# Attention kernel: value products in bursts of three steps, maximum products of two heads on row halves of the array

## What is computed

```python
q = jnp.einsum('bsd,hdk->bhsk', x, wq)
k = jnp.einsum('bsd,hdk->bhsk', x, wk)
v = jnp.einsum('bsd,hdk->bhsk', x, wv)
scores = jnp.einsum('bhsk,bhtk->bhst', q, k) / jnp.sqrt(jnp.asarray(K, x.dtype))
probs = jax.nn.softmax(scores, axis=-1)
o = jnp.einsum('bhst,bhtk->bhsk', probs, v)
...
return jnp.einsum('bse,ed->bsd', concated, head_kernel)
```

## Time and profile before

| | |
|---|---|
| median of 3 runs | 5213.08 us (5210.68 to 5217.73) |
| the profiled execution, its span | 5214.6 us |
| PE busy | 4965.0 us (95%) |
| DVE busy | 3832.6 us (73%) |
| POOL busy | 2796.0 us (54%) |
| ACT busy | 2665.8 us (51%) |
| granted TensorE clock, mean | 0.980 |

### The profile page before, as it was taken

The page is one execution under the profiler, slowest core; times in us unless marked ns, Lnnn a source line. Parts: engine busy times, 40 slices in busy tenths (PEclk is TensorE's granted clock), DMA queues, the critical chain, the costliest instruction groups (busy, mean ns, idle before and its releaser), DMA issues. The chain is left out here.

```text
span 5214.6 us, 92843 instructions
## 1 busy us (share of the span) xinstructions
PE 4965.0 (95%) x25829; PEld 3227.2 (62%) x25829; DVE 3832.6 (73%) x8495; ACT 2665.8 (51%) x6408; POOL 2796.0 (54%) x1611
## 2 busy tenths in 40 slices
PE   5999999999999999999999999999999999999997
PEld 3556666666566666666666666666666656666666
DVE  5667768677776777777777776777867777677765
ACT  2664555555544545545455455455455554554542
POOL 0665555555555555555555555555555555555652
PEclk7999999999999999999999999999999999999998
DMA  1000000000000000000000000000000000000000
GB/s 39 6 10 7 6 16 6 11 7 6 16 6 10 7 10 11 6 11 11 10 6 6 10 11 11 7 6 16 6 11 7 6 16 6 10 6 10 6 1 14
DMA packets 43025, 49.54 MB, mean 10 GB/s; under 512 B 26256, under 2 KB 34311, under 8 KB 42503
## 3 DMA queue, kind: packets, MB, share of 16 engines
q1 hardware_dynamic: 42503, 43.12, 2.7%
HBM read 23.45 MB, written 19.09 MB: 8 GB/s over the span
## 5 line engine op out<-in xcount | busy, mean ns | idle before, releaser
L1155 POOL TENSOR_TENSOR sums<-sums,probs 128x736 f32<-128x736 f32 (+3 forms) x1344 | 2384.6, 1774 | 1278.0 <-ACT probs L867 1262.6
L867 ACT ACTIVATE probs<-scores 128x368 f32<-128x368 f32 (+3 forms) x3456 | 1460.1, 474 | 1922.0 <-PE scores L761 1814.5
L925 DVE TENSOR_REDUCE part_max<-work 128x1 f32<-128x368 f32 (+3 forms) x3456 | 1657.3, 527 | 310.1 <-PE work L675 288.3
L778 PE MATMUL o_ps<-probs,values 128*64 128x368 f32 (+1 forms) x6912 | 1455.7, 500 | 0.0
L759 PE MATMUL scores<-q_a,k_a 128*128 128x368 f32 (+3 forms) x3456 | 1170.2, 339 | 61.1 <-issue 41.5
L761 PE MATMUL scores<-q_b,k_b 128*128 128x368 f32 (+3 forms) x3456 | 1146.4, 332 | 0.0
L675 PE MATMUL work<-k_a,q_a 128*128 128x368 f32 (+3 forms) x3456 | 1089.6, 378 | 48.0 <-DVE part_max L925 24.4
L675 PEld LDWEIGHTS work<-k_a,q_a 128*128 128x128 f32 (+1 forms) x3456 | 578.3, 184 | 777.4 <-issue 624.1
L1151 POOL TENSOR_TENSOR sums<-probs 128x736 f32<-128x736 f32 (+1 forms) x192 | 343.6, 1789 | 863.5 <-ACT probs L867 861.5
L759 PEld LDWEIGHTS scores<-q_a,k_a 128*128 128x128 f32 (+1 forms) x3456 | 639.5, 185 | 83.8 <-issue 33.2
L761 PEld LDWEIGHTS scores<-q_b,k_b 128*128 128x128 f32 (+1 forms) x3456 | 641.3, 186 | 53.0 <-issue 33.7
(11 more groups left out here) (186 smaller groups left out, 5039.6 us busy)
## 6 DMA issues: line engine op xcount, KB each, us to landing
resid_rows<-h_in SPq DMA_DIRECT2D x16, 576.0 KB, 2.8
h_out<-resid_rows SPq DMA_DIRECT2D x16, 576.0 KB, 4.1
h_in<-in_pe_table_dram SPq DMA_DIRECT2D x16, 512.0 KB
out_dram<-h_out SPq DMA_DIRECT2D x16, 512.0 KB
q_b<-max_rows SPq DMA_DIRECT2D x128, 4.0 KB
q_b<-max_rows SPq DMA_DIRECT2D x128, 0.3 KB
counts<-in_x_dram SPq DMA_DIRECT2D x16, 116.0 KB, 3.0
out_raw<-n_expert_out_weight_dram SPq DMA_DIRECT2D x1, 1024.0 KB
```

Source lines behind the costliest of these rows:

```text
L778: mm = nc.tensor.matmul(o_ps[64 * i:64 * i + 64, 0:cw], values[0:n, t, h * DH:(h + 1) * DH], probs[0:n, s % NP, i, 0:cw], start=(t == 0), ...
L867: nc.scalar.activation(probs[0:n, s % NP, i, 0:cw], scores[0:n, h % SB, 0:cw], ACT.Exp, scale=DH ** -0.5).then_inc(probs_ready, 1)
L925: nc.vector.tensor_reduce(part_max[0:n, i * NT + j, c:c + 1], w[0:n, 0:keys], AX.X, ALU.max).then_inc(drained[k], 1)
L1155: nc.gpsimd.tensor_tensor(acc, acc, probs[0:n, s % NP, :, 0:cw], ALU.add).then_inc(sums_done, 1)
```

## The change

- **Bursts.** `weigh` is no longer done in each step, but at every third step for the three steps before, twelve records in a row (`BURST`). `probs` has 5 buffers for that: the first two steps of a group of three alternate between two buffers each, the third always has the fifth.
- **Maxima in pairs.** A unit `max` is now both heads of a query tile and a key chunk: head 0 on rows 0 to 63 of the array, head 1 on rows 64 to 127, with the high parts alone, into two neighbouring banks. DVE reads both with one reduction (27 for each pair of heads in place of 54). `q_a` of the second head is laid out with its halves exchanged, so that its high part is in rows 64 to 127.
- **Their places.** Maxima no longer fill in: the three key chunks of one query tile stand at every third step, two units in front of the burst, one behind it (and behind a `sum`, which stands right after the burst). They start at step 15 of the pair before the one ahead. For every three query tiles there is now a `maxrow` and its own DMAs (2, 2 and 4 for the three groups), and `score` waits at the first step of each chunk for those groups that it needs.
- **Banks.** The four banks are given to the unit that finds one longest unused; a `max` takes banks 0 and 1 or 2 and 3.
- **Rest.** `qk` stands at every second step, `sum` one step later, ACT's copy of `o_ps` one step later; `h_in` shares memory with the last pair's `heads_t`, and `beats` with `logits`, to make room.

```diff
+SLOTS = LANES + LANES // 2
-NP = 3
+NP = 5
+GROUP = 3
-MAXROW = 23
+BURST = ("burst",)
+MAX_FIRST, MAX_EARLY = 15, 2
+MAX_DMAS = (2, 2, 4)
...
-LOAD = {"v": (48, 0, 36), "qk": (48, 95, 130), "max": (16, 50, 0), "maxrow": (10, 50, 0), "sum": (65, 0, 36),
+LOAD = {"v": (48, 0, 36), "qk": (48, 95, 130), "max": (17, 91, 0), "maxrow": (10, 50, 0), "sum": (65, 0, 36),
...
+    first = STEPS * (p - 1) + MAX_FIRST
+    return [(first + NT * g + GROUP * k, ("max", p, g, 3 * g + k, c))
+            for g in range(NC) for k in range(3) for c in range(NC)]
+
+
+def max_rows_at(p, g):
+
+    return STEPS * (p - 1) + MAX_FIRST + NT * g + 2 * GROUP + 2
...
-            put(NT * (q + 1) + 2, ("sum", q))
+            put(NT * (q + 1) + 3, ("sum", q))
...
+def in_order(units, burst):
+
+    pairs = [u for u in units if u[0] == "max"]
+    sums = [u for u in units if u[0] == "sum"]
+    others = [u for u in units if u[0] not in ("max", "sum")]
+    early = MAX_EARLY if burst else 0
+    return pairs[:early] + [BURST] * burst + sums + pairs[early:] + others
...
+            if u[0] == "max":
+                lane = min((0, 2), key=lambda k: max(used_at[k:k + 2]))
+                slot, lanes = LANES + lane // 2, (lane, lane + 1)
+            else:
+                lane = min(range(LANES), key=lambda k: used_at[k])
+                slot, lanes = lane, (lane,)
...
+    def slot(s):
+
+        return s // GROUP % 2 * 2 + s % GROUP if s % GROUP < GROUP - 1 else NP - 1
+
+    def held(s):
+
+        return GROUP if s % GROUP == GROUP - 1 else 2 * GROUP
...
-                mm = nc.tensor.matmul(w[0:n, 0:cw], q_a[p % 2][i][:, j * P:j * P + n],
-                                      k_a[p % 2][i][:, c0:c0 + cw], start=True, stop=True)
+                for i in range(2):
+                    rows_i = slice(DH * i, DH * i + DH)
+                    mm = nc.tensor.matmul(work[0:n, seg.lane[u] + i, 0:cw], q_a[p % 2][i][rows_i, j * P:j * P + n],
+                                          k_a[p % 2][i][rows_i, c0:c0 + cw], start=True, stop=True)
...
-            if s % STEPS == 0:
-                pe.wait_ge(max_loaded, 64 * (PAIRS * b + p + 1))
+            if t == 0:
+                pe.wait_ge(max_loaded, 16 * sum(MAX_DMAS) * (PAIRS * b + p) + 16 * sum(MAX_DMAS[:c + 1]))
...
+        def weigh(seg, it, b, s):
+
+            for done in range(s - GROUP, s):
+                weigh_one(seg, it, b, done)
...
-                wait(act, probs_used, ALL * b + s - NP + 1)
-                if not isinstance(b, int) or b > 0 or s >= NP:
-                    wait(act, sums_done, (NT - 1) * PAIRS * NC * b + summed(s - NP))
+                back = held(s)
+                wait(act, probs_used, ALL * b + s - back + 1)
+                if not isinstance(b, int) or b > 0 or s >= back:
+                    wait(act, sums_done, (NT - 1) * PAIRS * NC * b + summed(s - back))
...
-                nc.vector.tensor_reduce(part_max[0:n, i * NT + j, c:c + 1], w[0:n, 0:keys], AX.X,
+                lane = seg.lane[u]
+                nc.vector.tensor_reduce(part_max[0:n, :, j, c], work[0:n, lane:lane + 2, 0:keys], AX.X,
                                         ALU.max).then_inc(drained[k], 1)
```

212 lines of the change are left out of this document (112 added, 100 removed).

## The result

| | before | after |
|---|---|---|
| median, us | 5213.48 | **5619.76** (5617.80 to 5633.43) |
| profiled execution: span, us | 5214.6 | 5617.3 |
| PE busy | 4965.0 (95%) | 4780.4 (85%) |

The changed kernel takes 1.0784 times as long, 95% interval 1.0768 to 1.0799: 7.8% slower, where 5.7% faster was forecast, and outside the range. PE is busy for 185 us less and is done 403 us later.

What follows compares the result with a forecast made beforehand. The prediction took PE, busy 95%, to bound the kernel: 5214.6 - 477 of work on PE + 180 of waits = 4918, and 4916 us as the median lies 1.5 lower. The range was 4790 to 5100.

Steps and rivals of the forecast that it cites:

- Work on PE: All of PE's products and shape switches: 442 - 230 + 279 - 14 = 477 us off, 30 us an item.
- The visit's 0.35 us: Value products and sums on column halves: 0.15 us to enter, 0.20 to leave; 1264 fewer visits, 442 us off.
- the switches of 0.20 on either side: Full array to row halves and back around a burst: at least 0.40 us a burst, 230 us on over 576 bursts.
- the pair's overlap: Maximum products: both row halves run at once, a pair takes 0.175 us; 279 us off.
- rival 1: Weights of the row halves come one after another, pairs 0.22 us and bursts at 0.62; 5086 us; chance 15%.
- rival 4: Slower: the row halves don't overlap, a pair takes 0.336 us and the shape is dear; 5267 us; chance 6%.
- the gate's wait: Steps 21 to 27 of an item: PE waits 4.5 us for DVE, busy with the gate's chain and pairs' reductions.
- Together 12 us an item, 180 in all: Sum of new waits of PE, over 15 items with the full mix: gate 4.5, DVE elsewhere, DMAs, scores.
- DVE elsewhere: DVE late behind an embedding, an expert or a projection's four subtractions: 3 us an item, from none to 6.
- scores 2.5: In otherwise empty steps PE outpaces ACT's exponentials (0.67 against 0.84 us): eight groups or so, 0.3 each, an item.
- The DMAs' 2: Scores wait for the rows of maxima to be copied and land: 2 us an item, from none to 4.
- rival 2: DVE and the DMAs bind more: waits of 23 us an item in place of 12; 5086 us; chance 12%.

Runs made afterwards that it cites:

- e4: The changed kernel with DVE's reduction of a pair of maxima reading only 46 of the 368 keys; 5455 us.
- e10: The changed kernel with the pair's reduction reading an eighth of the keys and ACT's exponential taking only the first half of the queries; 5397 us.
- e6: The changed kernel with bursts of three steps kept, but maxima as before the change, and half of a burst step's units ahead of the burst; 5242 us.
- e13: Against e6: four bursts in nine steps (of 3, 2, 2 and 2 steps) in place of three, the plan's load of a burst in proportion; 5190 us.
- e7: The changed kernel with value products of one step at every step again, pairs of maxima still at every third step; 5835 us.
- e16: The changed kernel with its pairs of maxima one to a step in place of three at each third step, the maxima's row written one step later; 5691 us.
- e17: Against e16: the bursts and even plan of e15 besides, so pairs of maxima stand one to a step; 5621 us.
- e15: Against e6: four bursts in nine steps (of 3, 2, 2 and 2 steps), and the plan counts 80 at each step; 5140 us.
- e18: Against e15: ten of an item's twelve sums stand one step later, right behind a burst; 5162 us.
- e14: Against e6: the plan counts 80 at each step in place of 240 at each third, bursts unchanged; 5227 us.
- e1: The changed kernel with one pair of maxima in front of a burst and two behind it; 5489 us.
- e2: The changed kernel with all three pairs of maxima behind the burst; 5691 us.
- e8: The changed kernel with one pair ahead of a burst, projections moved to burst steps where they may be, and put ahead of the burst there; 5392 us.
- e12: Against e6: all other units of a burst step put ahead of the burst; 5273 us.

## Why the prediction was wrong

- **Work on PE: right.** 477 us off forecast, 488 measured. The visit's 0.35 us, the burst's 2.0, the switches of 0.20 on either side, the pair's overlap (some 4 ns between its ends) and its 0.37: each within 0.02 us. Rivals 1 and 4 are refuted by the pair's records. (In rival 1, 1728 pairs of 0.22 are 380 us and not 387, so its time would be 5079; nothing rests on it.)
- **The single costs that I worked out for other engines: right too.** A pair's reduction 0.9 us (911 ns); the gate's wait 4.5 (4.0, a group earlier).
- **The waits: wrong, and this is the step that failed.** "Together 12 us an item, 180 in all" was 750 us, and 900 with the clock. Its terms by item, against measured ones, which hold the low clock of their places: DVE elsewhere 3, against some 31 (35 more in front of maxima, less the gate's 4); scores 2.5, against 16; value products, which had no term, 5. The low clock had no term either and is 10 of these (150 over 15 items). The DMAs' 2 came to nothing: the weight loads of the scores waited for `q_b<-max_rows` once, for 1.1 us.
- **The reasoning in it that failed** is "235 us on DVE against 270 or so of work on PE. On the whole it fits." That is a comparison of throughputs. e4 and e10 show that throughput isn't what most of the waits are for: with DVE at 48% of busy time 892 and 822 of 975 us remain. The rows above show PE standing at one product while later ones that need nothing stand behind it, and a unit's bank read by a chain of 1.5 us (an expert's four evictions) to 2.5 (1.9 of a projection's casts, then a subtraction of 0.54).
- **What came in its place** has two parts. Before, value products of each step, 0.97 us with entry and exit, that need no bank, lay between a unit and the next use of its bank. I counted these as pure cost to be taken off, but they were cover: bursts alone bring 416 us of waits (e6), and shorter bursts give 197 back (e13). The pairs of maxima bring 410 us by themselves (e7), with value products in every step. One part of this is that three stand in one step (spread, the kernel has 327 us of waits less, e16); spread they still have 233 more than single maxima (e17 against e15).
- "Those lumps lie under a burst of 2 us" (against rival 2) was wrong as well: two of three pairs stand in front of the burst, where it covers nothing.
- **Rival 2** had the direction. Its price, 23 us an item, was less than half of 60, and its ground, slack on DVE, isn't what e10 shows. The one rival that came out slower, 4, did so by saving only 71 us of work; none that kept the 477 put more waits against them. The range ended where rival 1 and 2 did, since I bounded the unknown waits by single places and not by what the value products had been covering: some 1 us in each of two steps of three, 72 an item, which would have given 5213 - 477 + 15 x 72 = 5816. That it lies above the measured time is in part luck, since this sum has nothing for the pairs' own waits.
- The sign of what I wrote last was right: "I am wrong if ... PE's share of busy time falls under 90% though its work is as said." It is 85%.

What isn't settled: what the rest of the change (banks by longest unused, sums a step later), which is in e6 and in e7 alike, brings by itself; why bursts and pairs together bring 750 us of waits and not the 826 of the two alone; how much of e18's 75 us of new waits is the sums' own; and what part of the low clock would go by itself if the waits did. The tables show that the amount of waits alone doesn't decide it: with 635 to 650 us of waits the clock's part is 83 (e6), 136 (e17), 221 (e16) and 267 us (e7), the three high ones all with pairs.

## What to carry to other kernels

Work that needs no bank and no fresh result was cover here for the engine that ran it, so before lumping such work, count what each step between lumps has left to hide: price a unit's whole drain chain against PE's time until that bank is wanted again, step by step; busy shares over an item didn't show it. If a switch of array shape is dear, join fewer steps than you could: bursts of two and three steps were the only ones that paid (e13, e15, e18), those of three never did (e6, e14). Where units stand around a burst is to be tried out: one pair ahead was better than two or none (e1, e2), a projection ahead of it helped in e8, all units ahead cost 31 us in e12. And two products that run at once also hold two banks for one longer read; with four work banks, e17's pairs saved nothing beside e15 and cost 233 us of waits.

## What the runs showed of the hardware that I had not expected

- A change between the full array, column halves and row halves cost 0.20 us (0.36 to 0.37 us from end to end of the first full or paired product behind it, against 0.17 without), and 0.15 into column halves. Row halves took no more than a full product behind the same change, though both halves' weights are loaded anew. By "TensorEngine Tiling (Array Packing)", Key Properties, of the Trainium skill a change of mode drains the array; the trace agrees with 0.20 us a change.
- The clock: PE at 85% of busy time spent 485 us at 1.2 GHz, at 95% it spent 145. In the stretch shown it was low behind waits of 0.84 and 0.49 us, and a burst ran at half the pace (3.76 us for 2.08). 150 us of clock came with 750 us of waits. That the waits bring it down fits the stretch, but no run shows it apart, and e6 and e7 have the same waits with 83 and 267 us of clock.
- Shortening a read of banks helps less than in proportion: a reduction of 2 x 46 columns took 245 ns and one of 2 x 368 took 911 (or 904 in e17); an exponential of 184 columns 324 ns and one of 368 478. By the two sizes each reduction has some 150 ns and each exponential some 170 that don't depend on its length, an estimate.
